# Channel-mix stage: the subtraction moves from VectorE to GpSimd, and the PSUM tile `pr` gets a third slot

## The reference

```
y   = layernorm(x + attention(x))         # window of 256, 16 heads of 64, 2 key/value heads
y1  = y shifted by one row (zeros first)
xr  = mu_r*y + (1-mu_r)*y1                # = y1 + mu_r*(y - y1)
xk  = mu_k*y + (1-mu_k)*y1
r   = sigmoid(xr @ W_r.T)
k   = square(relu(xk @ W_k.T))
out = layernorm(y + r * (k @ W_v.T))
```

## Time and profile before

| | |
|---|---|
| time, median of 3 runs | 1073.72 us (1072.98 to 1075.09) |
| time of the profiled execution | 1076.05 us |
| its span (core 3, the slowest of 1066.0 to 1074.5) | 1074.5 us |
| busy: TensorE / VectorE / ScalarE / GpSimd | 591.4 / 308.6 / 264.2 / 54.7 us |
| channel mix, from the barrier to the end | about 757 to 1074.5 us |

### The profile page before, as it was taken

The page is one execution under the profiler, slowest core; times in us unless marked ns, Lnnn a source line. Parts: engine busy times, 40 slices in busy tenths (PEclk is TensorE's granted clock), DMA queues, the critical chain, the costliest instruction groups (busy, mean ns, idle before and its releaser), DMA issues. The chain is left out here.

```text
span 1074.5 us, 11465 instructions; the slowest of 8 cores (1066.0 to 1074.5 us)
## 1 busy us (share of the span) xinstructions
PE 591.4 (55%) x2834; PEld 224.9 (21%) x2834; DVE 308.6 (29%) x767; ACT 264.2 (25%) x720; POOL 54.7 (5%) x69
## 2 busy tenths in 40 slices
PE   0077556515465666665566566554086384583782
PEld 0032223101121222221212222211032131231330
DVE  0022112101323323223333232333513616507304
ACT  0011001501333333223323332330021140330322
POOL 2000000100000000000000000000011020030030
PEclk9998778655666666666666666756588698797897
DMA  9944642896332233343232323342500130120101
GB/s 124 136 75 75 103 64 45 128 172 125 65 79 68 61 78 65 64 74 78 66 69 60 79 64 63 76 79 44 98 1 1 49 79 1 75 53 7 72 1 78
DMA packets 178142, 75.05 MB, mean 70 GB/s; under 512 B 165920, under 2 KB 166048, under 8 KB 178080
## 3 DMA queue, kind: packets, MB, share of 16 engines
q1 hardware_dynamic: 165248, 48.37, 22.8%
q0 software_dynamic: 12832, 25.96, 13.3%
HBM read 43.01 MB, written 8.39 MB: 48 GB/s over the span
## 5 line engine op out<-in xcount | busy, mean ns | idle before, releaser
L502 ACT ACTIVATE p<-psc,konst 128x384 bf16<-128x384 f32 x272 | 155.9, 578 | 350.5 <-PE psc L490 339.5
L570 PE MATMUL po<-pt,vt 128*64 128x128 bf16 x408 | 63.0, 288 | 184.1 <-DMA pt<-p16n 184.1
L484 PE MATMUL psc<-maskq,ident 128*128 128x384 bf16 x272 | 105.1, 423 | 36.0 <-ACT p L502 31.2
L607 PE MATMUL pwo<-w16o,ao 128*128 128x512 bf16 x272 | 100.8, 537 | 22.5 <-DVE ao L590 22.5
L930 PE MATMUL pr<-w16vf,kact 128*128 128x512 bf16 x256 | 67.4, 430 | 69.3 <-DVE g L944 56.3
L590 DVE CAST ao<-po 128x512 bf16<-128x512 f32 x34 | 23.5, 692 | 242.4 <-PE po L575 242.4
L867 PE MATMUL pr<-w16r,xr 128*128 128x512 bf16 x256 | 61.6, 401 | 51.2 <-DVE xk L845 32.3
L570 PEld LDWEIGHTS po<-pt,vt 128*64 128x64 bf16 x408 | 36.0, 141 | 219.4 <-issue 219.4
L296 PE MATMUL paP<-xfm,w16k 128*128 128x512 bf16 x40 | 17.7, 621 | 97.5 <-DMA xfm<-x16t 97.5
L529 DVE TENSOR_SCALAR p16n<-p,rall 128x384 bf16<-128x384 bf16 x272 | 65.4, 310 | 0.2 <-issue 0.2
L575 PE MATMUL po<-pt,vt 128*64 128x128 bf16 x408 | 64.6, 292 | 0.0
(11 more groups left out here) (68 smaller groups left out, 521.7 us busy)
## 6 DMA issues: line engine op xcount, KB each, us to landing
x<-xpad POOLq DMA_DIRECT2D x17, 512.0 KB, 3.6
out<-out SPq DMA_DIRECT2D x16, 512.0 KB, 2.6
x16t<-xpad POOLq DMA_DIRECT2D x5, 1024.0 KB, 10.9
pt<-p16n SPq DMA_TRANSPOSE x136, 2.8
w16q<-wq POOLq DMA_DIRECT2D x1, 2048.0 KB, 32.7
w16o<-wo POOLq DMA_DIRECT2D x1, 2048.0 KB, 16.6
w16r<-wr POOLq DMA_DIRECT2D x1, 2048.0 KB, 30.1
w16kf<-wkf POOLq DMA_DIRECT2D x1, 2048.0 KB, 42.4
```

Source lines behind the costliest of these rows:

```text
L484: e.matmul(psc[:, HH % 3, 0:WIN], ident[:, :], maskq[:, :], start=True, stop=False)
L502: e.activation(p16[:, tau % 2, h, :], psc[:, H % 3, 0:WIN], AF.Exp, bias=konst[:, 0:1], accum_out=sall[:, h:h + 1]).then_inc(bEX.sem, 1)
L570: last = e.matmul(po[0:64, slot * 128:(slot + 1) * 128], lhs, pt16[:, slot_a, c * 128:(c + 1) * 128], start=(c == 0), stop=(c == 2), tile_ ...
L607: e.matmul(pwo[:, nh * 512:(nh + 1) * 512], ao16[:, tau % 2, kc, :], w16o[:, kc, nh * 512:(nh + 1) * 512], start=(kc == 0), stop=False)
```

## The change

Three things change, all in the channel mix.

- The subtraction goes to GpSimd's queue (function `fsub`), with a semaphore of its own, `cSUB`. The subtractions of a group stand on GpSimd behind the squares of the group before.
- `d16` has two slots. Subtraction number n waits for the end of chunk n-2 (`cMXV`), and VectorE's chunk n waits for subtraction n (`cSUB`). VectorE's waits for its own instructions inside the mix are gone.
- `pr` has three slots instead of two; a tile waits for the reader of tile `pru - 3`. With `pk` this fills PSUM.

```diff
-        nc.sbuf_tensor("d16", [128, 512], BF16) as d16,
+        nc.sbuf_tensor("d16", [128, 2, 512], BF16) as d16,
-        nc.psum_tensor("pr", [128, 2, 1024], F32) as pr,
+        nc.psum_tensor("pr", [128, 3, 1024], F32) as pr,
...
+                vsub = cSUB.post()
+                def fsub(e, G=G, par=par, chx=chx, vte=vte_all, vsub=vsub):
+                    wtok(e, *vte)
+                    if vsub > 2:
+                        e.wait_ge(cMXV.sem, vsub - 2)
+                    e.tensor_sub(d16[:, chx % 2, :], yfm[:, par, chx, 16:528],
+                                 yfm[:, par, chx, 15:527]).then_inc(cSUB.sem, 1)
+                mix_s.emit("gpsimd", fsub)
...
-                    if chx >= 1 or G >= 1:
-                        e.wait_ge(cMXV.sem, vmx - 1)
-                    dsync = sfV.post()
-                    e.wait_ge(sfV.sem, dsync - 1)
-                    e.tensor_sub(d16[:, :], yfm[:, par, chx, 16:528],
-                                 yfm[:, par, chx, 15:527]).then_inc(sfV.sem, 1)
-                    e.wait_ge(sfV.sem, dsync)
...
+                    e.wait_ge(cSUB.sem, vsub)
+                    e.scalar_tensor_tensor(xr16[:, chx, :], d16[:, chx % 2, :],
...
-                war = pr_toks.get(pru - 2)
+                war = pr_toks.get(pru - 3)
...
+                tprev.q["gpsimd"] = tprev.q["gpsimd"] + mix_s.q["gpsimd"]
```

More of the change, by code:

```diff
@@ L768, in build_nc @@
         cMXV = Chan(nc, cst, "cMXV")
+        cSUB = Chan(nc, cst, "cSUB")
         cMXG = Chan(nc, cst, "cMXG")
@@ L825, in build_nc, with fmx @@
             for chx in range(NCHUNK):
+                vsub = cSUB.post()
[6 more added lines that the diff above has]
+                mix_s.emit("gpsimd", fsub)
                 vmx = cMXV.post()
-                def fmx(e, G=G, par=par, chx=chx, vte=vte_all, vmx=vmx):
-                    wtok(e, *vte)
+                def fmx(e, G=G, par=par, chx=chx, vsub=vsub, vmx=vmx):
                     if G >= 1 and chx == 0:
@@ L831, in fmx @@
                         e.wait_ge(cWK.sem, 8 * G)
-                    if chx >= 1 or G >= 1:
-                        e.wait_ge(cMXV.sem, vmx - 1)
-                    dsync = sfV.post()
-                    e.wait_ge(sfV.sem, dsync - 1)
-                    e.tensor_sub(d16[:, :], yfm[:, par, chx, 16:528],
-                                 yfm[:, par, chx, 15:527]).then_inc(sfV.sem, 1)
-                    e.wait_ge(sfV.sem, dsync)
-                    rsync = sfV.post()
-                    e.scalar_tensor_tensor(xr16[:, chx, :], d16[:, :],
+                    e.wait_ge(cSUB.sem, vsub)
+                    e.scalar_tensor_tensor(xr16[:, chx, :], d16[:, chx % 2, :],
                                            mur_s[:, chx:chx + 1],
                                            yfm[:, par, chx, 15:527],
-                                           ALU.mult, ALU.add).then_inc(sfV.sem, 1)
-                    e.wait_ge(sfV.sem, dsync)
-                    e.scalar_tensor_tensor(xk16[:, chx, :], d16[:, :],
+                                           ALU.mult, ALU.add)
+                    e.scalar_tensor_tensor(xk16[:, chx, :], d16[:, chx % 2, :],
                                            muk_s[:, chx:chx + 1],
@@ L866, in fwr @@
                         for kc in range(NCHUNK):
-                            last = e.matmul(pr[:, pru % 2, nh * 512:(nh + 1) * 512],
+                            last = e.matmul(pr[:, pru % 3, nh * 512:(nh + 1) * 512],
                                             xr16[:, kc, ts * 128:(ts + 1) * 128],
@@ L878, in fsg @@
                         e.wait_ge(cG.sem, 4 * G)
-                    e.activation(r16[:, ts, :], pr[:, pru % 2, :], AF.Sigmoid) \
+                    e.activation(r16[:, ts, :], pr[:, pru % 3, :], AF.Sigmoid) \
                         .then_inc(cSG.sem, 1)
@@ L943, in fg @@
                         e.wait_ge(cZ2.sem, 4 * G + ts)
-                    e.tensor_mul(g32[:, :], pr[:, pru % 2, :], r16[:, ts, :]) \
+                    e.tensor_mul(g32[:, :], pr[:, pru % 3, :], r16[:, ts, :]) \
                         .then_inc(cG.sem, 1)
```

## The result

The changed kernel takes 1055.13 us (median of 9 runs, 1052.24 to 1063.9) beside 1073.9 us for the kernel before on the same chips; the ratio is 0.983, 95% interval 0.980 to 0.985. It is 1.7% faster. The forecast was 0.4% faster, 1069 us, with a range of 1038 to 1077 us.

What follows compares the result with a forecast made beforehand. The prediction took a chain through VectorE's channel mix and the way from first sigmoid to k tiles as the bound. Its terms, -10.4 + 3.0 + 3 x 1.0 = about -4.4 us, gave about 1069 us from 1073.7, range 1038 to 1077.

Steps and rivals of the forecast that it cites:

- the unknown overlap: Channel mix: whether GpSimd's subtractions run beside VectorE's instructions (22.7 us off) or take turns (about 6 us more).
- The third slot: Between first sigmoid and first k tile, groups 1 to 3: one r tile leaves the chain, 10.4 us off.
- One at a time: Channel mix: GpSimd's subtractions and VectorE's instructions exclude each other; about 6 us more in all.
- rival 1: Channel mix: GpSimd and VectorE run side by side, mix 22.7 us off, total 1040.6 us; chance 22%.
- The stretched rows: Sign of turns in the mix: subtractions longer than 1.04 us or idle before them, xr or xk longer than 0.75.
- the mixes of 17 to 18.5 us, and of 20 for group 0: Sign of turns: how long a later group's mix and group 0's mix would take.
- The size of a turn: Channel mix: two chunks cost two subtractions of 1.04 us, four VectorE instructions and 0.2 for engine changes, 5.04 us.
- rival 2: Channel mix: one subtraction, then one chunk, both hand-overs each time, 2.76 us a chunk; 1075.4 us; chance 13%.
- rival 3: Subtraction on GpSimd costs more than the square's 1.04 us; at 1.5 us each, 1081 us; chance 12%.
- The clock: TensorE's r tile 3 could fall to the 1.2 GHz level; counted 0, at most 5.1 us lost.
- The sum: Whole kernel: 10.4 us off by the slot, 3.0 and 3 x 1.0 more by the mixes, about -4.4 us.

Runs made afterwards that it cites:

- slot_only: The kernel before with the third slot of pr alone, subtraction still on VectorE: 1064.3 us, ratio 0.988 to the kernel before.
- gp_memset: The changed kernel with GpSimd's subtraction replaced by a memset of the same d16 slot: 1041.3 us, ratio 0.967 to the kernel before.
- mix_first: The changed kernel with all eight subtractions early on VectorE, eight slots, and xr and xk ahead of the first g: 1031.6 us, ratio 0.960 to the kernel before.
- ve_stagger: The changed kernel with the subtractions back on VectorE, each one chunk ahead, two slots of d16: 1057.0 us, ratio 0.984 to the kernel before.
- gp_ahead: The changed kernel with eight slots for the subtraction's result, so GpSimd can run ahead: 1049.6 us, ratio 0.976 to the kernel before.
- ve_idle: The changed kernel with all eight subtractions of a group on VectorE in its idle time behind the copy, eight slots: 1047.4 us, ratio 0.975 to the kernel before.
- slot_warm: slot_only with 12 extra matmuls in the gap before each group's first v tile: 1062.2 us, ratio 0.986 to the kernel before.
- mix_warm: mix_first with 12 extra matmuls before the fourth r tile of groups 1 to 3: 1026.7 us, ratio 0.955 to the kernel before.

## Why the forecast came out as it did

The measured 1055.1 us lies in the stated range, but that range (1038 to 1077) was wide enough for either end of the unknown overlap, and the forecast's own range (1065 to 1074) missed. The change is 18.8 us, more than four times the 4.4 us forecast. One of its two terms was right, the other had the wrong sign, and a third gain was not foreseen.

- *The third slot.* Forecast 10.4 us; slot_only shows 10.3, the place is the one named, and the first relu moved with the first k tile. Right.
- *One at a time.* Of the two ends for GpSimd and VectorE, the chosen one was the true one: rival 1 (side by side, 1040.6 us) would have been a mix of 11 us; it was 15.3, and gp_memset shows what side by side would look like. The stretched rows came as named; the mixes of 17 to 18.5 us, and of 20 for group 0, did not.
- *The size of a turn.* This is the term that was wrong. I priced a contended subtraction at 1.04 us and 0.1 for the change of turn, so that the mixes came out 6 us dearer in all. It holds VectorE up for 0.78 us: 0.26 us of its 1.04 lie outside the time in which it keeps VectorE waiting. With 0.78 instead of 1.14 the same sum gives 15.7 us for a later mix; the last 0.4 us are chunks of 1.33 us, which I had at 1.38. Measured: 15.3 instead of 17.9 us for a later mix (three times 2.6 us) and 17.2 instead of 20.2 for group 0, 4.8 us less than before instead of 6 more, 10.8 us of difference. The sign of the whole term hung on this one price.
- *Strict alternation* (rival 2) described the order: one subtraction, one chunk. Its price (2.76 us a chunk, measured 2.11) was wrong for the same reason, and because the hand-overs cost nothing: the subtraction arrives while `xr` still runs, and its result is wanted only a chunk later.
- *A dearer subtraction* (rival 3) was out: 1.0 us alone, like the square.
- *The clock.* I counted 0, with 5.1 us of loss as the other end. It was a gain of up to 5.0 us, at another tile than the one I looked at: the first v tile, slow in three places of four before. I had no bound on the side of a gain. Why these tiles got the full clock is open, so this part of the result is luck and not design.
- *The sum.* Forecast -4.4; with 10.8 by the turn and up to 5.0 by the clock: -15.2 to -20.2; measured -18.8 in the time.

## What to carry to other kernels

Moving an instruction from VectorE to GpSimd does not gain all of its VectorE time. Here, where GpSimd read SBUF and VectorE's instructions had two SBUF inputs, the engines took turns; what counts then is how many of the moved instructions fall outside the time in which VectorE works, and how long each of the others holds VectorE up (here 0.78 of 1.04 us). Look first for idle time on VectorE itself, or for a queue order that takes the work off the chain: with three slots of `pr`, the same three instructions a chunk, all on VectorE, took the kernel from 1064.3 us (slot_only, ratio 0.988) to 1031.6 us (mix_first, 0.960) by their place and by eight slots for `d`, which allow it. A PSUM slot is worth what stands between its release and the next link of the chain, and no more: 3.45 us here, three times, not the wait of 18 us that the profile named. And a shorter stage can be paid back elsewhere: in ve_stagger, gp_ahead, ve_idle and gp_memset most or all first v tiles were slow, at 1.2 to 2.9 us each.

## What the runs showed of the hardware

- A GpSimd tensor_tensor beside a VectorE instruction with two SBUF inputs: the later one waits for the earlier (rows of 1.42 instead of 1.04 us and of 1.52 instead of 0.75, with the wait inside them and no idle time in front). A GpSimd memset beside the same: nothing (0.52 and 0.75 us). A GpSimd subtraction beside `g`, with one input in PSUM and one in SBUF: nothing (1.00 and 1.22 us, gp_ahead).
- TensorE behind equal gaps of 3.25 us ran its next 16 matmuls at a granted clock of 1.00 or of 0.70 (2.4 GHz all along, or 1.2 GHz for a part). What made it so here is open: the slow places changed from one arrangement to the next. With 12 matmuls in the gap, the tile behind it was at the full clock in all places: the four first v tiles (slot_warm) and the three fourth r tiles (mix_warm), on all eight cores.
